# A Perceiver block on one core: the context turned by transposing DMAs in place of TensorE, another order of the first four steps, low parts by GpSimd

## The reference

```python
# x (2, 256, 256), ctx (2, 4096, 256), w_q/w_k/w_v (256, 1024), w_o (1024, 256)
q = (layernorm(x) @ w_q) ; k = (ctx @ w_k) ; v = (ctx @ w_v)      # 16 heads of 64
attn = softmax(q k^T / 8) ; x = x + (attn v) @ w_o
x = x + hyperbolic_attention(layernorm(x)) ; x = x + experts(layernorm(x))
```

## Time and profile before

| | us |
|---|---|
| median of 3 runs | 1123.02 (1120.26 to 1123.82) |
| the profiled execution: its time | 1124.97 |
| its span, first to last instruction | 1123.3 |
| PE / DVE / ACT / POOL busy | 1051.4 / 810.9 / 796.4 / 680.1 |
| step 0 begins, step 1 begins | 50.3, 112.8 |

### The profile page before, as it was taken

The page is one execution under the profiler, slowest core; times in us unless marked ns, Lnnn a source line. Parts: engine busy times, 40 slices in busy tenths (PEclk is TensorE's granted clock), DMA queues, the critical chain, the costliest instruction groups (busy, mean ns, idle before and its releaser), DMA issues.

```text
span 1123.3 us, 36747 instructions
## 1 busy us (share of the span) xinstructions
PE 1051.4 (94%) x15493; PEld 789.3 (70%) x15493; DVE 810.9 (72%) x1059; ACT 796.4 (71%) x1452; POOL 680.1 (61%) x614
## 2 busy tenths in 40 slices
PE   5899999999999999999999999999999999666688
PEld 3477777777777777777777777777777777543466
DVE  3887777777777777777777777777767759457442
ACT  4776776777777777777777777777776756798854
POOL 3665666666666666666666666676665556734233
PEclk9999999999999999999999999999999999787799
DMA  9100000000000000000000000003000010000000
GB/s 329 51 2 16 7 17 7 17 6 17 7 16 7 17 7 17 7 16 8 17 7 16 8 16 7 16 8 119 7 2 7 28 52 3 2 1 1 1 1 20
DMA packets 27381, 25.45 MB, mean 23 GB/s; under 512 B 1850, under 2 KB 25938, under 8 KB 27218
## 3 DMA queue, kind: packets, MB, share of 16 engines
q1 hardware_dynamic: 27218, 23.10, 6.5%
HBM read 22.57 MB, written 0.52 MB: 21 GB/s over the span
## 4 chain that ended last, share of the span: by engine, by line
PE 81%; DVE 8%; issue 4%; ACT 4%; POOL 2%; DMA 1%; SPq 0%; ACTq 0%; POOLq 0%; DVEq 0%
PE ps L1359 15%; PE ps L1330 14%; PE ps L1443 13%; PE ps L1390 6%; PE ps L1491 5%; PE ps L1486 5%; PE ps L1489 5%; PE ps L1431 4%; PE ps L759 2%; PE ps L719 2%; POOL psums L2048 2%; PE ps L1422 1%; PE ps L1316 1%; DVE m_part L1849 1%; PE ps L535 1%
## 5 line engine op out<-in xcount | busy, mean ns | idle before, releaser
L2048 POOL TENSOR_TENSOR psums<-probs 128x512 f16<-128x512 f32 x512 | 590.1, 1172 | 317.5 <-ACT probs L1686 264.2
L1677 ACT ACTIVATE probs<-ps 128x512 f32<-128x512 f32 x512 | 279.7, 600 | 199.2 <-PE ps L1443 198.3
L1849 DVE TENSOR_REDUCE m_part<-ps 128x2 f32<-128x1024 f32 x256 | 313.2, 1224 | 142.8 <-PE ps L1390 142.7
L1686 ACT ACTIVATE probs<-probs 128x512 f16<-128x512 f32 x384 | 242.1, 632 | 0.3
L1443 PE MATMUL ps<-q_hi,k_p 64*128 64x256 f16 x2048 | 211.1, 269 | 0.0
L1486 PE MATMUL ps<-v_sb,probs 128*128 128x65 f16 x2048 | 205.9, 193 | 4.5 <-POOL psums L2048 4.5
L1489 PE MATMUL ps<-v_sb,probs 128*128 128x64 f16 x2048 | 205.8, 192 | 0.0
L1491 PE MATMUL ps<-v_sb,psums 128*128 128x65 f16 x2048 | 205.4, 194 | 0.0
L1486 PEld LDWEIGHTS ps<-v_sb,probs 128*128 128x128 f16 x2048 | 188.4, 98 | 19.0 <-POOL psums L2048 6.1
L1489 PEld LDWEIGHTS ps<-v_sb,probs 128*128 128x128 f16 x2048 | 188.0, 97 | 15.6
L1491 PEld LDWEIGHTS ps<-v_sb,psums 128*128 128x128 f16 x2048 | 188.2, 97 | 0.0
(11 more groups left out here) (246 smaller groups left out, 1704.4 us busy)
## 6 DMA issues: line engine op xcount, KB each, us to landing
ctx_hi<-in_L_ffn_W_dram SPq DMA_DIRECT2D x2, 2048.0 KB, 9.7
wqk_raw<-in_L_xattn_w_q_dram SPq DMA_DIRECT2D x16, 128.0 KB, 2.3
wqk_raw<-in_L_xattn_w_k_dram SPq DMA_DIRECT2D x16, 128.0 KB, 2.5
probs<-in_ctx_dram SPq DMA_DIRECT2D x4, 512.0 KB, 7.4
wv_raw<-in_L_xattn_w_v_dram SPq DMA_DIRECT2D x16, 128.0 KB, 2.5
k_p<-in_ctx_dram SPq DMA_DIRECT2D x4, 512.0 KB, 9.2
wo_raw<-in_L_xattn_w_o_dram SPq DMA_DIRECT2D x16, 128.0 KB, 2.1
ctx_hi<-in_ctx_dram SPq DMA_DIRECT2D x7, 256.0 KB, 7.0
```

What stands on the lines that cost most here:

```text
L1677: nc.scalar.activation(p_raw[:, s:s + 2, h, :], ps[:, score_bank(n, pair, h), :].rearrange("p (k q) -> p k q", k=2), ACT.Exp, scale=XSCALE ...
L1686: nc.scalar.activation(p_hi[:, s % NP, :, :], p_raw[:, s % NX, :, :], ACT.Copy) \
L1849: nc.vector.tensor_reduce(m_part[:, j, t, :], ps[:, bank:bank + 2, :], AX.X, ALU.max) \
L2048: nc.gpsimd.tensor_tensor(p_lo[:, s % NP, :, :].rearrange("p h q -> p (h q)"), p_raw[:, s % NX, :, :].rearrange("p h q -> p (h q)"), p_hi[ ...
```

## The change

**The turning.** A chunk of the context is now split as it lies, tokens in partitions: ACT rounds it to fp16 (`split_context_high`), POOL subtracts (`split_context_low`), both into `nat`, eight slots (`NAT`) in what was spare memory. A DMA that transposes, issued by SP, writes each part turned into `ctx_hi` or `ctx_lo` (`turn_context`): two per chunk, 128 partitions by 1024 fp16 numbers, 256 KB each. No PE transposes of the context are left, and `ctx_hi`/`ctx_lo` are laid out by chunks.

**The prologue.** The loads of batch 0's context go out from ACT's queue, ahead of ACT's work; SP issues the transposes. ACT splits four chunks ahead (`LEAD`). The low part of the first step's keys, which DVE made from PSUM, is now made by PE (`subtract_high`: minus the high part is added in PSUM, a product with `minus`) and copied by ACT (`take_low_k`). POOL's constants (`tail_constants`) move from the end of the prologue to its beginning.

**The steps.** `ORDER` begins (0,0), (1,0), (0,1), (1,1), head pair first: two steps on batch 0, so that batch 1 is first projected in step 1 (`FIRST1 = 2`). Its six later chunks are split in halves in 12 periods (`SPLIT_AT`: all 8 of step 0, the first 4 of step 1): in each one ACT copy of 128x512 at the period's start and one POOL subtraction of 128x512 ahead of POOL's third weight tile. SP turns chunks 2 to 4 before its loads for step 2, and 5 to 7 after them.

```diff
-ORDER = tuple((i // 2, i % 2) for i in range(STEPS - 6)) + tuple(
+ORDER = ((0, 0), (1, 0), (0, 1), (1, 1)) + tuple((i // 2, i % 2) for i in range(4, STEPS - 6)) + tuple(
     (hp, b) for b in range(B) for hp in range(HP - 3, HP))
...
-LATER_AT = {q: q + EARLY for q in range(KCH - EARLY)}
+EARLY = 2
+SPLIT_AT = {g: (KCH + EARLY + g // 2, g % 2) for g in range(2 * (KCH - EARLY))}
+NAT = 8
+LEAD = 4
...
+        def split_context_high(act, i, halves=(0, 1)):
...
+            parts = raw_parts(i)
+            for raw, tiles in [parts[h] for h in halves if h < len(parts)]:
+                last = nc.scalar.activation(nat_part(i, 0, tiles), raw, ACT.Copy)
...
+        def split_context_low(eng, ops, i, halves=(0, 1)):
...
+            for raw, tiles in [parts[h] for h in halves if h < len(parts)]:
+                last = ops.tensor_tensor(nat_part(i, 1, tiles), raw, nat_part(i, 0, tiles), ALU.subtract)
...
+            def turn_context(i, low):
...
+                if low:
+                    low_done(i)
+                else:
+                    sp.wait_ge(s_th, i + 1)
+                    if b == 1 and u >= 1:
+                        low_done(i - 1)
+                sp.dma_start((ctx_hi, ctx_lo)[low][:, b, u, :, :].rearrange("p c (t k) -> p (c t) k", t=CS),
+                             nat[:, i % NAT, low, :], transpose=True).then_inc((s_dh, s_dl)[low][i % NAT], 16)
+
+            turn_context(0, 0)
+            for u in range(1, KCH + 1):
+                if u < KCH:
+                    turn_context(u, 0)
+                turn_context(u - 1, 1)
+                if u - 1 in (3, 5):
+                    load_context((u - 4) // 2)
+            for u in range(2, KCH):
+                load_context(u)
+                if u in (3, 5):
+                    turn_context(KCH + u // 4, 0)
+                    turn_context(KCH + u // 4, 1)
...
             for n in range(STEPS):
+                if n == 2:
+                    for u in range(EARLY, KCH - 3):
+                        turn_context(KCH + u, 0)
+                        turn_context(KCH + u, 1)
                 step(n)
+                if n == 2:
+                    for u in range(KCH - 3, KCH):
+                        turn_context(KCH + u, 0)
+                        turn_context(KCH + u, 1)
...
+            def subtract_high(j):
+
+                pe.wait_ge(s_kh, j + 1)
+                pe.matmul(ps[:, (PV, PK)[j % 2], :], minus[:, :], k_p[:, 0, 0, 512 * j:512 * (j + 1)],
+                          start=False, stop=True, skip_group_check=True).then_inc(s_kn, 1)
...
+            for j in range(KCH):
+                if j + 1 < KCH:
+                    for part in range(2):
+                        project_first_k(j + 1, part)
+                subtract_high(j)
+                maxima(2 * j, 0, 0)
+                maxima(2 * j + 1, 0, 0)
```

More of the change, by code:

```diff
@@ L246, in perceiver @@
         s_xc = sem("s_xc")
-        s_tp = sem("s_tp")
         s_th = sem("s_th")
         s_tl = sem("s_tl")
-        s_cx = sem("s_cx")
-        s_ch = sem("s_ch")
-        s_cl = sem("s_cl")
+        s_dh = [sem(f"s_dh{i}") for i in range(NAT)]
+        s_dl = [sem(f"s_dl{i}") for i in range(NAT)]
+        s_kn = sem("s_kn")
+        s_t2 = sem("s_t2")
+        s_t3 = sem("s_t3")
         s_wkh = sem("s_wkh")
@@ L1522, in step @@
                         project_v(0, n + 1, 1 - par, ORDER[n + 1][1], MX)
-                    if first and q in LATER_AT:
-                        transposes_later(q, LATER_AT[q], 0)
                     if n == DONE0 and q in TURN_IN:
@@ L1534, in step @@
                     pv_before(n, q, (0, 1))
-                    if first and q in LATER_AT:
-                        transposes_later(q, LATER_AT[q], 1)
                     if q == Y_IN and 0 < n < STEPS - 2:
@@ L1707, in step @@
                         take_v(0, n + 1, MX)
-                    if first and q in LATER_AT:
-                        context_later(LATER_AT[q], 0)
                     if n == DONE0 and q in TURN_IN:
@@ L1714, in step @@
                     high(n, s + 3)
-                    if first and q in LATER_AT:
-                        context_later(LATER_AT[q], 1)
                     if q == OT_IN and not first:
@@ L1750, in last_step @@
                     beside(2 * pair + 1)
+            chunks = ctx.rearrange("b (n p t) c -> b n p t c", p=P, t=8)
+            for u in range(KCH):
+                tiles = slice(4 * (u % 2), 4 * (u % 2) + 4)
+                act.dma_start(stage[u // 4][:, u // 2 % 2, tiles, :], chunks[0, u // 2, :, tiles, :]) \
+                    .then_inc(s_ctx[u], 16)
             root_of_variance(act, 0, slice(0, NT))
             split_k(0, 0)
-            context(0)
+            split_context_high(act, 0)
+            split_context_high(act, 1)
             act.wait_ge(s_xt, NC)
@@ L1986, in _ @@
             normalised(0, slice(0, NT))
[L1987 to L1990 removed]
+            take_q(0)
+            for j in range(KCH):
+                maxima(2 * j, 0)
+                if j == 3:
                     split_v(0, 0)
[L1992 removed]
+                if j == 4:
                     split_k(1, 1)
[L1994 to L2001 removed]
+                maxima(2 * j + 1, 0)
+            take_q(1)
             take_max(0)
```

229 lines of the change are left out of this document (104 added, 125 removed).

## The result

The changed kernel takes 1132.68 us (median of four executions, 1132.0 to 1137.1) against 1122.97 for the kernel before: ratio 1.0106, interval 1.0085 to 1.0127. By the medians the change makes the kernel 9.7 us slower. I had forecast 1115.

A forecast was written before the change was run, and what follows sets the result against it. PE was taken to bound the kernel from step 1 on, with prologue and step 0 looser. Gains of 6.8 us in the prologue and 1.2 in steps 0 and 1 took 8.0 off 1123.3: 1115, range 1109 to 1139.

The forecast's parts named there:

- predicted start: End of the prologue: step 0 begins at 43.5 us in place of 50.3, 6.8 us gained.
- When it begins: Prologue: x lands 0.5 us later from sharing the DMAs; SP's third high part is issued at 14.0 us.
- What a transposing DMA costs: Prologue: transposes taken at 1.4 us each in SP's queue, between 0.67 and 2.7; step 0 then begins at 43.5 us.
- X: Time SP's queue needs for each transposing DMA when one stands behind another, taken as 1.4 us.
- rivals with 2.7 and 3.8 us: Prologue, slower: transposes one at a time, 1131 us, chance 0.19; each 128x128 block on its own, 1144 us, chance 0.13.
- The floor of 2.44 us a chunk: Prologue: if transposes keep up, DVE's two maxima set the pace at 2.44 us a chunk; step 0 begins at 42.9.
- The tail: Prologue's end: from the last low part to step 0 takes 7.9 us, the same work as before.
- Step 0's transposes: Periods 0 to 5 of step 0: without PE's transposes, 0.91 us each, six periods gain 5.0 us.
- The ring of POOL and ACT: The 12 split periods: POOL's extra subtraction makes a 7.0 us cycle against PE's 6.64; 3.8 us lost.
- no ring: Steps 0 and 1: POOL's subtraction fits its idle time, or ACT's exponentials pass; 5.0 gained, time 1111, chance 0.15.
- Order, layout, queue: Steps: new step order, chunk-wise layout and SP's later transposes cost nothing, hidden if each transpose takes below 3 us.

The follow-up runs named there:

- Experiment 2: The kernel before with only batch 0's context loads moved from SP's to ACT's queue: 1127.39 us, ratio 1.005.
- experiment 4: The changed kernel with DVE normalising x before it takes the low part of the first key weights: 1130.38 us, ratio 1.0074.
- experiment 1: The changed kernel with batch 0's context loads back on SP's queue, behind x and the first weights: 1133.16 us, ratio 1.0099.
- Experiments 5: The early version: the changed kernel with its prologue reordered, loads over both queues, normalising first, queries ahead of first keys: 1131.43 us, ratio 1.0082.
- experiment 6: The early version with plain copies of the same bytes in place of all transposing DMAs, context left unturned: 1124.6 us, ratio 1.001.
- experiment 8: The changed kernel with each half's low part in the 12 periods shared, one tile by POOL, one by DVE: 1130.69 us, ratio 1.0067.
- experiment 11: The changed kernel with the prologue of the kernel before, and low parts in the 12 periods shared by POOL and DVE: 1119.1 us, ratio 0.996.
- experiment 10: The changed kernel with the prologue of the kernel before, TensorE turning batch 0 and two chunks of batch 1: 1125.27 us, ratio 1.0026.
- Experiment 7: The early version with only the low parts' DMAs made plain copies, high parts still transposed: 1129.54 us, ratio 1.0061.

## Why the prediction was wrong

The predicted start was 43.5 us, by the landmark of the earlier trace rows; it came at 58.95, 15.4 later. The steps were to gain 1.2 and lost 0.6. Step by step:

*"When it begins": the step that failed most.* 14.0 was predicted for the third high part, 24.14 measured: **10.1 of the 15.4 us**. I had allowed x 0.5 us for sharing the DMA engines with the eight loads. It was 2.9 us late (its statistics began at 4.50 in the timeline of before and at 7.39 now), and I hadn't asked after the key weights at all: 11.32 us from issue to landing. `xn` began at 16.82 and not at 8.45, 8.4 late: 6.5 of waiting for the weights, which DVE's order put ahead of it, and 1.8 for `rstd` beside POOL. Then `xn` itself took 1.8 longer beside POOL, whose work there is the change's own, and PE's transposes of x took 1.94 in place of 1.51. 8.4 + 1.8 + 0.4 less the 0.5 allowed is 10.1. Experiment 2 shows the loads' part alone in the kernel before, 4.0 us of start; experiment 4 shows 2.6 us for DVE's order. A term that I had put at 0.5 us, x's landing, and one that I had put at nothing, the weights' landing, were the failure; the theory that the loads alone make the loss didn't hold either (experiment 1).

*"What a transposing DMA costs": the number right, its meaning wrong.* X was 1.39 (1.34 of issue) against the 1.4 taken. That the number fits is luck, as it was a middle between bounds that lay four times apart. The rivals with 2.7 and 3.8 us are refuted; that the first of them had step 0 begin at 59.1 and the time at 1131, close to what came, is luck too. But I had priced it as time of SP's queue and left the 16 DMA engines out: by the share of busy time a transpose fills them for about as long, 256 KB in 1.39 us is 189 GB/s, where the earlier trace rows has 391 for loads. So four loads aren't 0.52 us each, they come on top at the engines; issues block (2.12 for one, 3.77 for two), and landing took 3.3 and 4.5 us on the chain in place of 2.7. From the third high part to the product of the last low part I had 45.7 - 24.1 = 21.6 with the measured start put in; it was 49.2 - 24.1 = 25.1: **3.5 us**. Only 2.0 of them are the transposes': the last low part is issued at 44.5 and lands 3.2 later, at 47.7 for 45.7. The other 1.5 are the wait of its product for a key bank, the floor of the next paragraph. Experiments 5 and 6 show what transposing costs in the early version's prologue: 7.3 us of start against copying the same bytes. The Trainium skill, "Advanced Engine Details and Errata", section on the X-bar transpose, says that transposes are as fast as plain DMAs; the trace disagrees for these 256 KB from SBUF to SBUF, 1.34 us of issue against 0.47 to 0.60, and a DMA share of 1.02 at 207 GB/s against 0.66 at 219. The 1309 ns that the Trainium skill gives for one block of 128x128 by DMA, in "VectorE: DVE Perf Modes", "The three transpose paths", don't add up block by block: the trace shows eight blocks in 1.39 us when transposes follow each other.

*The floor of 2.44 us a chunk.* It isn't DVE's but that of PE and ACT on the two key banks, 2.65 us a chunk. I had counted ACT's 2.2 us as work and not seen that two of the copies stand between PE's products. So even with free copies the prologue would not have gained 7.4 us: experiment 6 begins at 50.3, after an early beginning that the changed kernel doesn't have.

*The tail.* 7.9 us were taken over from before; from the last low part's product to step 0 it was 58.95 - 49.2 = 9.8: **1.9 us**. PE's queries and first keys for step 1 (1.99 and 2.07) stand behind the last maxima there. The granted clock was 0.81 from 52 to 54 us and 0.50 from 54 to 56, the lower of its two levels (1.2 and 2.4 GHz), after PE had been busy 1.20 of the 2 us before. In the early version, where it was 1.00 from 52 to 56 us, the same work took 1.06 and 1.29, so the clock is most of the 1.9.

10.1 + 3.5 + 1.9 = 15.5, which is the prologue's miss of 15.4.

*Step 0's transposes.* Right: six periods of 7.24 to 7.50 us in the kernel before are 6.64 each where nothing else holds them (four of the six in experiment 8), 4.7 us for the 5.0 predicted.

*The ring of POOL and ACT.* Right in mechanism: 6.9 us a period for 7.0. In size, POOL's whole subtractions cost 3.3 us in all (experiment 8 against the changed kernel) for 3.8, but only 1.8 of them are the ring. The rival "no ring" is refuted. What I had missed is the end of step 0. There DVE's small operations on vectors of one number per partition (`rvec`) stand on the path, beside POOL. In the changed kernel:

```profile
109.16 1.05 DVE L1043 TENSOR_TENSOR rvec<-rvec 128x1 f32<-128x1 f32 x1
...
111.54 1.15 DVE L1052 TENSOR_TENSOR rvec<-rvec 128x1 f32<-128x1 f32 x1
```

```profile
107.93 2.27 POOL L2081 TENSOR_TENSOR psums<-probs 128x512 f16<-128x512 f32 x2
111.52 1.15 POOL L2081 TENSOR_TENSOR psums<-probs 128x512 f16<-128x512 f32 x1 [1.32 <-ACT probs L1722]
```

Operations of 0.16 us take 1.05 and 1.15, 1.9 us together, and the last period of step 0 is 12.31 us from exponential to exponential, where it was 10.43. In experiments 8 and 11 only one of them is held (0.55 in all) and it is 10.81. So the steps, predicted at 1.2 gained, lost 0.6: 4.7 gained by the transposes, 3.3 lost to POOL's whole subtractions (1.5 of them here, 12.31 - 10.81), and 2.0 that experiment 8 loses as well. Of these 0.4 lie at this boundary, 0.7 in step 1, 0.5 at the start of step 0 (its first exponential comes 2.1 us behind the row maxima, 1.6 before: ACT's copy for the split stands between them, which the prediction had put at nothing), and 0.4 in two periods in which weights are split.

*"Order, layout, queue": nothing.* Right, as far as the runs show. The steps from 2 on take 55.0 us each as before, and in step 1 of experiment 8 the excess lies in periods with a split or next to one; its last three, 6.64, 7.48 and 6.74 us, are as before. No run changes the order alone.

**What a single profile can say.** Step 13 takes 60.2 to 60.6 us in some profiles and 61.8 to 62.3 in others (the kernel before 60.6, the changed one 60.2, experiment 10 62.3, experiment 11 60.2). No edit touches it and it goes with no start of step 0. It goes with the granted clock: that was 1.00 over step 13 in all seven profiles up to 60.6 us, and 0.97 in all six above. In experiment 10 PE was busy 0.17 of the 2 us from 820, and from 824 to 826 the granted clock was 0.50. It limits what a single profile can say of a total to about 2 us.

**What stays open.** That the DMA engines' fullness and not the order of one queue holds the transposes up was shown by the share of busy time, not by an experiment with less traffic. Experiment 7, with half of the transposes, leaves both possible.

## What to carry to other kernels

A DMA that replaces an engine's work has two prices: its queue's issue time and the time of the 16 DMA engines, which everything else that loads at that moment pays too; add up the second over the stretch before moving work there. When loads move to another queue, follow the small transfers on which the first chain hangs (here x and the key weights) and not just the moved ones. A step freed on one engine is worth only what the next ring allows, so work out the bank ring (product, copy, copy) and POOL's ring before the busy times.

## What the runs showed of the hardware

- **Transposing DMAs from SBUF to SBUF** of 128x1024 fp16, one behind the other, took 1.33 to 1.34 us of issue each, began 1.39 us apart, and landed in 3.3 and 4.5 us on the chain; as plain copies they took 0.47 to 0.60 of issue. With transposes a full DMA side moved 194 to 209 GB/s, with loads 391.
- **An issue can block for long**: two transposes behind 4 MB of loads in the same queue held SP 8.80 us.
- **A small operation of DVE waits out POOL's operation.** The operation at 111.54 ends at 112.69, and POOL's at 112.67; that at 109.16 is held until POOL's end at 110.20; `rstd` at 14.79 ends at 16.79, when POOL's first subtraction of 2.12 us does. One number per partition costs 1.05 or 1.15 us in place of 0.16, and `rstd`'s four cost 2.00. The Trainium skill, "GPSIMD Engine Reference", section "Specifications", says that GpSimd shares its SBUF interfaces with VectorE, with contention for instructions with two SBUF inputs or in a 2-port mode. The trace agrees for these operations, which have two inputs in SBUF, and adds the size for them: until the end of the instruction under way.
- **The same work of PE at two granted clocks**: values and keys at the end of step 0 took 2.60 and 1.78 us at 0.61, and 1.45 and 1.34 at 1.00, in two profiles whose instructions there are the same (the kernel before and experiment 2).
